# Pairwise products of features: tiles of 128 batch rows, stores of 31,744 B a partition, and the loads on ScalarE's queue

## The chip, the core and the metric

The kernel runs on one core of a Trainium2 chip. The metric is the device time of one execution in microseconds (us). The core has TensorE (PE; its weight loads are PEld), VectorE (DVE), ScalarE (ACT), GpSimd (POOL), SyncE (SP), and 16 DMA engines that move data between HBM and the on-chip memory. SBUF and PSUM have 128 partitions.

## The reference, cut to what matters

```python
# x: (B, F, E) = (2048, 32, 64) float32, W: (64, 64) float32
i_idx, j_idx = jnp.triu_indices(32, k=1)          # 496 pairs, i < j, i outermost
xw = jnp.einsum('bfe,ed->bfd', x, W)
y = xw[:, i_idx, :] * x[:, j_idx, :]              # (2048, 496, 64)
```

x has 16.8 MB and y has 260.0 MB. One batch row of y is 496 * 64 * 4 = 126,976 B.

## The kernel before

The 2048 batch rows are cut into 8 tiles of 256 rows; a partition holds two rows (`ROWS = 2`), row r * 128 + p of the tile for r = 0, 1. x_sb and xw_sb have two buffers each. The 496 pairs of a tile are cut into 16 chunks of 31 pairs, and `out_ring` has 8 slots of one chunk each: two rows of 31 * 64 * 4 = 7,936 B a partition, 2,031,616 B a slot.

SP issues every load and every store from one queue (lines 109 to 147). A load of a tile is three DMAs (line 112) for the features 0 to 7, 8 to 15 and 16 to 31 (`CUTS`): 2,048, 2,048 and 4,096 B in a row of x. The loads of tiles 0 and 1 come first; the load of tile t + 2 is issued behind the 16 stores of tile t. Each store (line 118) waits for the count `chunk_ready` and covers 256 stretches of 7,936 B in HBM. The first chunk of tile 0 is stored in two pieces (line 132), so that the first piece needs only part of x.

PE transposes two features at a time into PSUM (line 161), ACT copies that into `xT_sb` (line 202), PE multiplies it with W (line 174) and ACT copies the product into `xw_sb` (line 208), in groups of two features and two rows: 16 groups a tile. ACT also issues the two loads of W (line 221). After each tile but the first, ACT waits until VectorE has done the tile before, since xw_sb has two buffers.

VectorE multiplies (line 234): for each i, xw[i] broadcast over the features j > i, written into a slot of the ring. One instruction covers both rows; a chunk's end cuts an instruction in two. Before each chunk VectorE waits until the slot's last store has landed (`stored`).

Of the kernel before, what the change touches and what calls it, by code (L numbers as in the profile page):

```python
# [5 lines left out]
ALU = mybir.AluOpType  # L6
# [3 lines left out]
ROWS = 2  # L10
GROUP = 2
SLOTS = 8
CUTS = (0, 8, 16, 32)


def pair_pieces(F, chunk_pairs):

    chunks = [[] for _ in range(F * (F - 1) // 2 // chunk_pairs)]  # L20
    at = 0
    for i in range(F - 1):
        j = i + 1
        while j < F:
            place = at % chunk_pairs
            n = min(F - j, chunk_pairs - place)
            chunks[at // chunk_pairs].append((i, j, n, place))
            at += n
            j += n
    return chunks  # L30


def pairwise_interaction_kernel(nc: bass.Bass, x: bass.AP, W: bass.AP, out: bass.AP):
# [6 lines left out]


    B, F, E = x.shape
    PAIRS = F * (F - 1) // 2
    TILES = B // (LANES * ROWS)
    GROUPS = F // GROUP
    CHUNK = F - 1
    CHUNKS = PAIRS // CHUNK
    LAPS = CHUNKS // SLOTS
    PARTS = len(CUTS) - 1
    EARLY = CUTS[-2] - 1  # L50
    chunks = pair_pieces(F, CHUNK)
    assert B % (LANES * ROWS * 2) == 0 and PAIRS % CHUNK == 0 and CHUNKS % SLOTS == 0
    BANK = 512
    assert 2 * E == LANES and ROWS * GROUP * E <= BANK and F % GROUP == 0 and TILES >= 4
    assert CUTS[0] == 0 and CUTS[-1] == F and all(cut % GROUP == 0 for cut in CUTS)

    x_tiles = x.rearrange("(t r p) f e -> t p r f e", p=LANES, r=ROWS)
    out_tiles = out.rearrange("(t r p) q e -> t p r (q e)", p=LANES, r=ROWS)

    with ExitStack() as ctx:  # L60
# [6 lines left out]
        def sem(name):  # L67
            return ctx.enter_context(nc.semaphore(name))


        x_sb = [sb(f"x_sb{n}", [LANES, ROWS, F, E]) for n in range(2)]
        xw_sb = [sb(f"xw_sb{n}", [LANES, ROWS, F, E]) for n in range(2)]
        out_ring = [sb(f"out_ring{n}", [LANES, ROWS, CHUNK * E]) for n in range(SLOTS)]
        W_sb = sb("W_sb", [LANES, E])
        identity = sb("identity", [LANES, LANES])


        xT_sb = [sb(f"xT_sb{n}", [LANES, ROWS, GROUP // 2, LANES]) for n in range(2)]
        xT_ps = [psum(f"xT_ps{n}", [LANES, ROWS, GROUP // 2, LANES]) for n in range(2)]

        xw_bank = [[psum(f"xw_bank{n}_{odd}", [LANES, BANK]) for odd in range(2)] for n in range(2)]
        xw_ps = [[bank[:, 0:ROWS * GROUP // 2 * E].rearrange("p (r m e) -> p r m e", r=ROWS, e=E) for bank in banks]
                 for banks in xw_bank]
# [4 lines left out]
        x_landed = [[sem(f"x_landed{n}_{part}") for part in range(PARTS)] for n in range(2)]  # L88
# [5 lines left out]
        early_ready = sem("early_ready")  # L94
        early_stored = sem("early_stored")
        stored = [sem(f"stored{n}") for n in range(SLOTS)]

# [9 lines left out]
        @block.sync  # L107
        def _(sp):
            def load_x(t, buf):
                for part in range(PARTS):  # L110
                    f0, f1 = CUTS[part:part + 2]
                    sp.dma_start(x_sb[buf][:, :, f0:f1, :],  # L112
                                 x_tiles[t, :, :, f0:f1, :]).then_inc(x_landed[buf][part], 16)

            def store_chunk(t, c, skip=0):

                sp.wait_ge(chunk_ready, t * CHUNKS + c + 1)  # L117
                sp.dma_start(out_tiles[t, :, :, (c * CHUNK + skip) * E:(c + 1) * CHUNK * E],  # L118
                             out_ring[c % SLOTS][:, :, skip * E:]).then_inc(stored[c % SLOTS], 16)

            def store_then_load(k, buf, first=False):
                t = 2 * k + buf
                for c in range(CHUNKS):
                    store_chunk(t, c, skip=EARLY if first and c == 0 else 0)

                load_x(t + 2, buf)

            load_x(0, 0)
            load_x(1, 1)

            sp.wait_ge(early_ready, 1)
            sp.dma_start(out_tiles[0, :, :, 0:EARLY * E],
                         out_ring[0][:, :, 0:EARLY * E]).then_inc(early_stored, 16)
            for buf in range(2):
                store_then_load(0, buf, first=buf == 0)
            with sp.Fori(1, TILES // 2 - 1) as k:  # L136
                for buf in range(2):
                    store_then_load(k, buf)
            for t in range(TILES - 2, TILES):
                for c in range(CHUNKS):  # L140
                    store_chunk(t, c)

            sp.wait_ge(early_stored, 16)
            for slot in range(SLOTS):
                sp.wait_ge(stored[slot], 16 * TILES * LAPS)

        @block.tensor
        def _(pe):
            def tile(k, buf, first):
                t = 2 * k + buf  # L150

                def transpose_group(g):

                    if g * GROUP in CUTS:

                        pe.wait_ge(x_landed[buf][CUTS.index(g * GROUP)], 16 * (k + 1))
                    for r in range(ROWS):
                        for m in range(GROUP // 2):
                            f = g * GROUP + 2 * m
                            two = x_sb[buf][:, r, f:f + 2, :].rearrange("p f e -> p (f e)")  # L160
                            last = nc.tensor.transpose(xT_ps[g % 2][:, r, m, :], two, identity[:])  # L161
                    last.then_inc(transposed, 1)

                def project_group(g):

                    pe.wait_ge(xT_copied, t * GROUPS + g + 1)
                    if not (first and g < 2):

                        pe.wait_ge(xw_copied, 2 * (t * GROUPS + max(g - 1, 0)))
                    for r in range(ROWS):  # L170
                        for m in range(GROUP // 2):
                            for odd in range(2):
                                rows = slice(odd * E, (odd + 1) * E)
                                last = nc.tensor.matmul(xw_ps[g % 2][odd][:, r, m, :],  # L174
                                                        xT_sb[g % 2][rows, r, m, :], W_sb[rows, :],
                                                        start=True, stop=True)
                    last.then_inc(projected, 1)

                transpose_group(0)
                for g in range(GROUPS):  # L180
                    if g + 1 < GROUPS:
                        transpose_group(g + 1)
                    if first and g == 0:
                        pe.wait_ge(W_landed, 32)
                    project_group(g)

            pe.wait_ge(identity_ready, 1)
            for buf in range(2):
                tile(0, buf, first=buf == 0)
            with pe.Fori(1, TILES // 2) as k:  # L190
                for buf in range(2):
                    tile(k, buf, first=False)

        @block.scalar
        def _(act):
            def tile(k, buf, first):
                t = 2 * k + buf

                def copy_xT(g):

                    act.wait_ge(transposed, t * GROUPS + g + 1)
                    nc.scalar.copy(xT_sb[g % 2][:], xT_ps[g % 2][:]).then_inc(xT_copied, 1)  # L202

                def copy_xw(g):

                    act.wait_ge(projected, t * GROUPS + g + 1)
                    for odd in range(2):
                        nc.scalar.copy(xw_sb[buf][:, :, g * GROUP + odd:(g + 1) * GROUP:2, :],  # L208
                                       xw_ps[g % 2][odd]).then_inc(xw_copied, 1)

                copy_xT(0)
                for g in range(GROUPS):
                    if g + 1 < GROUPS:
                        copy_xT(g + 1)
                    copy_xw(g)
                if not first:

                    act.wait_ge(chunk_ready, t * CHUNKS)

            for odd in range(2):  # L220
                act.dma_start(W_sb[odd * E:(odd + 1) * E, :], W).then_inc(W_landed, 16)  # L221
            for buf in range(2):
                tile(0, buf, first=buf == 0)
            with act.Fori(1, TILES // 2) as k:
                for buf in range(2):
                    tile(k, buf, first=False)

        @block.vector
        def _(dve):
            def tile(k, buf, first):  # L230
                t = 2 * k + buf

                def multiply(slot, i, j, n, place):
                    return nc.vector.tensor_tensor(  # L234
                        slot[:, :, place:place + n, :],
                        xw_sb[buf][:, :, i:i + 1, :].to_broadcast([LANES, ROWS, n, E]),
# [54 lines left out]
```

## Time and profile before

| | |
|---|---|
| median of 3 runs | 672.33 us (672.03 to 672.47) |
| span of the profiled execution | 670.0 us |
| what lies around the span (median less span) | 2.3 us |
| VectorE busy | 562.1 us (84%) |
| PE busy | 211.4 us (32%) |
| ACT busy | 104.6 us (16%) |
| DMA, mean over the span | 413 GB/s |

The span runs from the first to the last instruction of the profiled execution; the profile gives this execution no other time of its own, so the runs' median stands for what lies around it. A window row of the trace gives, for a stretch of the span, each engine's busy time and number of instructions, TensorE's granted clock, the mean busy share of the 16 DMA engines and the rate at which they moved data. A share slightly above 1.00 means that packets of one engine overlap.

### The profile page before, as it was taken

How to read it: one execution, taken by the hardware profiler on the slowest of the kernel's cores; microseconds unless marked ns; L12 is line 12 of the kernel's file. 1: busy time of each engine (PE TensorE's matmuls, PEld its weight loads, DVE VectorE, ACT ScalarE, POOL GpSimd, SP SyncE). 2: the span in 40 equal slices, each digit the busy share in tenths (PEclk: the TensorE clock that was granted, in tenths of full speed). 3: DMA queues.
4: the chain of work that ended last, by engine and by line, in shares of the span. 5: the costliest groups of instructions: out<-in, count | busy, mean ns of one | idle time of the engine just before them, and what ended most of it. 6: DMA issues, size and time to landing. Idle time of an engine off the chain costs nothing.

```text
span 670.0 us, 4192 instructions
## 1 busy us (share of the span) xinstructions
PE 211.4 (32%) x1280; PEld 157.1 (23%) x1280; DVE 562.1 (84%) x362; ACT 104.6 (16%) x385; POOL 0.7 (0%) x6
## 2 busy tenths in 40 slices
PE   6995019400193001930029300392003910000000
PEld 4773017300173001720017200271002710000000
DVE  4999999999869997699977999779996899999800
ACT  3442004200042000410014100141001410000000
POOL 0000000000000000000000000000000000000000
DMA  8999999999999999999999999999999999999998
GB/s 318 422 416 419 418 360 427 425 427 429 381 426 426 426 429 373 426 428 428 427 382 428 426 429 427 382 427 427 429 425 396 428 426 428 425 420 419 419 420 342
DMA packets 41787, 277.00 MB, mean 413 GB/s; under 512 B 2608, under 2 KB 2608, under 8 KB 41776
## 3 DMA queue, kind: packets, MB, share of 16 engines
q1 hardware_dynamic: 41616, 276.83, 100.1%
q8 instruction: 5, 0.08, 0.0%
q10 hardware_dynamic: 160, 0.03, 0.0%
q14 instruction: 6, 0.05, 0.0%
HBM read 16.81 MB, written 260.05 MB: 413 GB/s over the span
## 4 chain that ended last, share of the span: by engine, by line
DMA 38%; SPq 29%; DVE 25%; issue 2%; DVEq 0%; PE 0%; ACTq 0%; ACT 0%
DMA out_dram<-out_ring 37%; DVE out_ring L234 25%; SPq L118 20%; SPq L112 8%; DMA W_sb<-in_W_dram 1%; DVEq L60 0%; SPq L117 0%; PE xw_bank L174 0%; ACTq L221 0%; ACT xw_sb L208 0%; SPq L136 0%; DVEq L250 0%; DVEq L267 0%; DVEq L242 0%; DVEq L254 0%
## 5 line engine op out<-in xcount | busy, mean ns | idle before, releaser
L234 DVE TENSOR_TENSOR out_ring<-xw_sb,x_sb 128x384 f32<-128x384 f32 (+11 forms) x362 | 562.1, 1615 | 73.6 <-DMA out_dram<-out_ring 64.3
L161 PE MATMUL xT_ps<-identity,x_sb 128*128 128x128 f32 x256 | 85.8, 444 | 325.7 <-DMA x_sb<-in_x_dram 325.7
L174 PE MATMUL xw_bank<-W_sb,xT_sb 64*128 64x64 f32 x1024 | 141.1, 430 | 1.9 <-DMA W_sb<-in_W_dram 1.2
L174 PEld LDWEIGHTS xw_bank<-W_sb,xT_sb 64*128 64x128 f32 x1024 | 118.7, 320 | 41.6 <-ACT xw_sb L208 25.4
L161 PEld LDWEIGHTS xT_ps<-identity,x_sb 128*128 128x128 f32 x256 | 38.4, 207 | 340.1 <-DMA x_sb<-in_x_dram 321.6
L202 ACT COPY xT_sb<-xT_ps 128x256 f32<-128x256 f32 x128 | 47.7, 373 | 344.7 <-PE xT_ps L161 344.2
L208 ACT COPY xw_sb<-xw_bank 128x128 f32<-128x128 f32 x256 | 55.6, 269 | 88.2 <-PE xw_bank L174 88.2
L202 ACT ACT_TABLE_LOAD x1 | 1.3, 1283 | 2.0 <-issue 2.0
L104 POOL TENSOR_SCALAR_AFFINE_SELECT identity<-identity 128x128 f32<-128x128 f32 x1 | 0.3, 294 | 0.2 <-POOL identity L102 0.2
L102 POOL MEMSET identity<- 128x128 f32 x1 | 0.2, 205 | 0.3 <-POOLq L279 0.3
L279 POOL MEMSET const-bfloat16-1.0<- 128x1 bf16 x1 | 0.1, 102 | 0.0
L279 POOL MEMSET const-uint8-127<- 128x1 uint8 x1 | 0.1, 102 | 0.0
L279 POOL MEMSET const-float32-0.0<- 128x1 f32 x1 | 0.1, 99 | 0.2 <-issue 0.2
L279 POOL MEMSET const-float32-1.0<- 128x1 f32 x1 | 0.1, 99 | 0.0
## 6 DMA issues: line engine op xcount, KB each, us to landing
out_dram<-out_ring SPq DMA_DIRECT2D x127, 1984.0 KB, 30.5
x_sb<-in_x_dram SPq DMA_DIRECT2D x16, 512.0 KB, 25.5
x_sb<-in_x_dram SPq DMA_DIRECT2D x8, 1024.0 KB, 22.7
out_dram<-out_ring SPq DMA_DIRECT2D x1, 1024.0 KB, 6.3
out_dram<-out_ring SPq DMA_DIRECT2D x1, 960.0 KB, 6.0
W_sb<-in_W_dram ACTq DMA_DIRECT2D x2, 16.0 KB, 5.4
```

The source lines that it names most:

```text
L102: nc.gpsimd.memset(identity[:], 0.0).then_inc(identity_zeroed, 1)
L104: nc.gpsimd.affine_select(out=identity[:], in_=identity[:], compare_op=ALU.not_equal, fill=1.0, base=0, pattern=[[-1, LANES]], channel_mul ...
L112: sp.dma_start(x_sb[buf][:, :, f0:f1, :], x_tiles[t, :, :, f0:f1, :]).then_inc(x_landed[buf][part], 16)
L118: sp.dma_start(out_tiles[t, :, :, (c * CHUNK + skip) * E:(c + 1) * CHUNK * E], out_ring[c % SLOTS][:, :, skip * E:]).then_inc(stored[c % S ...
L161: last = nc.tensor.transpose(xT_ps[g % 2][:, r, m, :], two, identity[:])
L174: last = nc.tensor.matmul(xw_ps[g % 2][odd][:, r, m, :], xT_sb[g % 2][rows, r, m, :], W_sb[rows, :], start=True, stop=True)
L202: nc.scalar.copy(xT_sb[g % 2][:], xT_ps[g % 2][:]).then_inc(xT_copied, 1)
L208: nc.scalar.copy(xw_sb[buf][:, :, g * GROUP + odd:(g + 1) * GROUP:2, :], xw_ps[g % 2][odd]).then_inc(xw_copied, 1)
L234: return nc.vector.tensor_tensor(slot[:, :, place:place + n, :], xw_sb[buf][:, :, i:i + 1, :].to_broadcast([LANES, ROWS, n, E]), x_sb[buf] ...
L279: nc = _bacc.Bacc("TRN2", target_bir_lowering=False, num_devices=1)
```

## The change

The batch is cut into 16 tiles of 128 rows, one row a partition. Rows are dealt to partitions differently: rows 2p and 2p + 1 of 256 go to partition p, so a load of 256 rows is 16,384 contiguous bytes a partition, and eight such loads (`LOADS`) fill four buffers (`XBUFS = 4`, eight tiles). The first load is two DMAs, one for each row of the pair. A tile's pairs are cut into 4 chunks of 124 pairs; the ring has 4 slots of 31,744 B a partition, and a store is 128 stretches of 31,744 B in HBM, whose starts lie 253,952 B apart. The stores stay on SP; all loads, the four at the start and the four later ones, are issued by ACT. A group is four features of one row (8 groups a tile). A multiply covers one row. PE waits for W before its first transpose; ACT raises `xw_copied` by 4 at the start so that PE's waits have one form. The piecewise start of the first chunk is gone. The loops of SP, ACT and VectorE are written out; PE's stays a loop.

```diff
-ROWS = 2
-GROUP = 2
-SLOTS = 8
-CUTS = (0, 8, 16, 32)
+ROWS = 2
+XBUFS = 4
+GROUP = 4
+CHUNKS = 4
+XW_PRIME = 4
...
-    x_tiles = x.rearrange("(t r p) f e -> t p r f e", p=LANES, r=ROWS)
-    out_tiles = out.rearrange("(t r p) q e -> t p r (q e)", p=LANES, r=ROWS)
+    x_loads = x.rearrange("(g p r) f e -> g p r f e", p=LANES, r=ROWS)
+    out_tiles = out.rearrange("(g p r) q e -> g r p (q e)", p=LANES, r=ROWS)
...
-        x_sb = [sb(f"x_sb{n}", [LANES, ROWS, F, E]) for n in range(2)]
-        xw_sb = [sb(f"xw_sb{n}", [LANES, ROWS, F, E]) for n in range(2)]
-        out_ring = [sb(f"out_ring{n}", [LANES, ROWS, CHUNK * E]) for n in range(SLOTS)]
+        x_sb = [sb(f"x_sb{n}", [LANES, ROWS, F, E]) for n in range(XBUFS)]
+        xw_sb = [sb(f"xw_sb{n}", [LANES, F, E]) for n in range(2)]
+        out_ring = [sb(f"out_ring{n}", [LANES, CHUNK * E]) for n in range(CHUNKS)]
...
         def _(sp):
+            for t in range(TILES):
+                g, r = divmod(t, ROWS)
                 for c in range(CHUNKS):
+                    sp.wait_ge(chunk_ready, t * CHUNKS + c + 1)
+                    sp.dma_start(out_tiles[g, r, :, c * CHUNK * E:(c + 1) * CHUNK * E],
+                                 out_ring[c][:]).then_inc(stored[c], 16)
...
         def _(act):
+            def load(g):
+                buf = g % XBUFS
+                if buf == 0:
                     for r in range(ROWS):
+                        act.dma_start(x_sb[0][:, r], x_loads[g, :, r]).then_inc(x_landed[0][r], 16)
+                else:
+                    act.dma_start(x_sb[buf][:], x_loads[g]).then_inc(x_landed[buf][0], 16)
...
+            for odd in range(2):
+                act.dma_start(W_sb[odd * E:(odd + 1) * E, :], W).then_inc(W_landed, 16)
+            for g in range(XBUFS):
+                load(g)
+            act.sem_inc(xw_copied, XW_PRIME)
+            for t in range(TILES):
+                copy_xT(t, 0)
+                if t >= 2:
+                    act.wait_ge(chunk_ready, (t - 1) * CHUNKS)
+                    done, r = divmod(t - 2, ROWS)
+                    if r == ROWS - 1 and done + XBUFS < LOADS:
+                        load(done + XBUFS)
                 for g in range(GROUPS):
                     if g + 1 < GROUPS:
+                        copy_xT(t, g + 1)
+                    copy_xw(t, g)
...
         def _(dve):
+            for t in range(TILES):
+                load, r = divmod(t, ROWS)
+                buf = load % XBUFS
                 for c in range(CHUNKS):
+                    if t > 0:
+                        dve.wait_ge(stored[c], 16 * t)
+                    slot = out_ring[c][:].rearrange("p (q e) -> p q e", e=E)
                     for i, j, n, place in chunks[c]:
+                        if i == 0 and r < len(x_landed[buf]):
+                            dve.wait_ge(x_landed[buf][r], 16 * (load // XBUFS + 1))
                         if i % GROUP == 0 and j == i + 1:
+                            dve.wait_ge(xw_copied, XW_PRIME + 2 * (t * GROUPS + i // GROUP + 1))
+                        last = nc.vector.tensor_tensor(
+                            slot[:, place:place + n, :], xw_sb[t % 2][:, i:i + 1, :].to_broadcast([LANES, n, E]),
+                            x_sb[buf][:, r, j:j + n, :], ALU.mult)
                     last.then_inc(chunk_ready, 1)
```

## Rows read from the trace of the kernel before

**Rows 1.** The page: span, and busy time of the engines (share of the span).

```profile
span 670.0 us, 4192 instructions
...
PE 211.4 (32%) x1280; PEld 157.1 (23%) x1280; DVE 562.1 (84%) x362; ACT 104.6 (16%) x385; POOL 0.7 (0%) x6
```

**Rows 2.** The page: all DMA packets, and the bytes read and written.

```profile
DMA packets 41787, 277.00 MB, mean 413 GB/s; under 512 B 2608, under 2 KB 2608, under 8 KB 41776
...
HBM read 16.81 MB, written 260.05 MB: 413 GB/s over the span
```

**Rows 3.** The chain that ended last, by engine.

```profile
DMA 38%; SPq 29%; DVE 25%; issue 2%; DVEq 0%; PE 0%; ACTq 0%; ACT 0%
```

**Rows 4.** Waits, all engines: total us, times, longest us.

```profile
DVE out_ring L234 <- DMA out_dram<-out_ring: 64.3, 89, 7.4
```

**Rows 5.** Windows without loads: last columns clock, DMA share, GB/s.

```profile
20.00:90.00 70.00, 39.15 (x242) 29.13 (x240) 70.00 (x46) 19.45 (x73) 0.00 (x0) 1.00 1.01 418
...
440.00:490.00 50.00, 16.43 (x104) 12.26 (x102) 46.93 (x34) 8.14 (x31) 0.00 (x0) 1.00 1.01 427
...
590.00:660.00 70.00, 0.00 (x0) 0.00 (x0) 42.04 (x33) 0.00 (x0) 0.00 (x0) 1.00 1.01 419
```

**Rows 6.** Windows around the six later loads.

```profile
90.00:100.00 10.00, 2.36 (x13) 1.85 (x14) 10.00 (x7) 0.83 (x3) 0.00 (x0) 1.00 0.98 322
170.00:180.00 10.00, 0.00 (x0) 0.00 (x0) 9.45 (x6) 0.00 (x0) 0.00 (x0) 1.00 0.99 353
250.00:270.00 20.00, 5.34 (x32) 4.06 (x32) 14.47 (x8) 2.36 (x8) 0.00 (x0) 1.00 1.00 383
340.00:350.00 10.00, 2.72 (x14) 1.94 (x14) 8.42 (x5) 1.18 (x4) 0.00 (x0) 1.00 0.97 356
420.00:430.00 10.00, 0.10 (x1) 0.10 (x2) 9.09 (x5) 0.00 (x0) 0.00 (x0) 1.00 0.98 349
500.00:510.00 10.00, 0.00 (x0) 0.00 (x0) 9.04 (x5) 0.00 (x0) 0.00 (x0) 1.00 0.98 379
```

**Rows 7.** Windows of one us, at the start, loads alone.

```profile
2.00:3.00 1.00, 0.00 (x0) 0.00 (x0) 0.00 (x0) 1.00 (x1) 0.00 (x0) 1.00 0.67 225
...
4.00:5.00 1.00, 0.00 (x0) 0.00 (x0) 0.00 (x0) 0.00 (x0) 0.00 (x0) 1.00 0.82 205
...
7.00:8.00 1.00, 0.51 (x6) 0.51 (x6) 0.00 (x0) 0.00 (x0) 0.00 (x0) 1.00 0.98 406
...
8.00:9.00 1.00, 1.00 (x8) 0.71 (x6) 0.00 (x0) 0.35 (x2) 0.00 (x0) 1.00 1.02 416
```

**Rows 8.** Windows of the start and of the end.

```profile
0.00:20.00 20.00, 13.60 (x82) 10.12 (x82) 10.88 (x6) 7.68 (x24) 0.70 (x6) 1.00 0.90 336
...
660.00:670.00 10.00, 0.00 (x0) 0.00 (x0) 0.00 (x0) 0.00 (x0) 0.00 (x0) 1.00 0.69 290
```

**Rows 9.** VectorE's multiplies, largest and a small form: busy, mean ns.

```profile
L234 DVE TENSOR_TENSOR out_ring<-xw_sb,x_sb 128x3968 f32<-128x3968 f32 x7 | 30.0, 4290 | 1.3 <-DMA out_dram<-out_ring 1.3
...
L234 DVE TENSOR_TENSOR out_ring<-xw_sb,x_sb 128x384 f32<-128x384 f32 x32 | 17.7, 554 | 3.8 <-DMA out_dram<-out_ring 3.8
```

**Rows 10.** Timeline of the start: start us, us, engine, line.

```profile
0.74 1.19 ACTq L221 DMA_DIRECT2D W_sb<-in_W_dram  x2
...
0.75 3.67 SPq L112 DMA_DIRECT2D x_sb<-in_x_dram  x6
...
1.96 1.28 ACT L202 ACT_TABLE_LOAD   x1 [1.96 <-issue]
...
5.21 1.09 PE L161 MATMUL xT_ps<-identity,x_sb 128*128 128x128 f32 x4 [5.21 <-DMA x_sb<-in_x_dram]
...
9.12 16.37 DVE L234 TENSOR_TENSOR out_ring<-xw_sb,x_sb 128x896 f32<-128x896 f32 x8 [9.12 <-ACT xw_sb L208]
```

**Rows 11.** One line's instructions, L118: the stores' issue.

```profile
L118 SPq DMA_DIRECT2D out_dram<-out_ring x128: 372/4201/9513, 13.6 to 637.5; - x128
```

**Rows 12.** The page's DMA issues: KB each, us to landing.

```profile
out_dram<-out_ring SPq DMA_DIRECT2D x127, 1984.0 KB, 30.5
```

More of the change, by code:

```diff
@@ L43, in pairwise_interaction_kernel @@
     PAIRS = F * (F - 1) // 2
-    TILES = B // (LANES * ROWS)
+    TILES = B // LANES
+    LOADS = TILES // ROWS
     GROUPS = F // GROUP
[L46 to L50, printed above, removed]
-    chunks = pair_pieces(F, CHUNK)
[L52 to L55, printed above, removed]
-    x_tiles = x.rearrange("(t r p) f e -> t p r f e", p=LANES, r=ROWS)
-    out_tiles = out.rearrange("(t r p) q e -> t p r (q e)", p=LANES, r=ROWS)
+    HALF = GROUP // 2
+    CHUNK = PAIRS // CHUNKS
+    LAP = XBUFS * ROWS
+    chunks = pair_pieces(F, CHUNK)
+    assert B % (LANES * ROWS) == 0 and PAIRS % CHUNKS == 0 and TILES % LAP == 0
+    assert 2 * E == LANES and F % GROUP == 0 and GROUP % 2 == 0 and GROUPS % 2 == 0
+    x_loads = x.rearrange("(g p r) f e -> g p r f e", p=LANES, r=ROWS)
+    out_tiles = out.rearrange("(g p r) q e -> g r p (q e)", p=LANES, r=ROWS)
     with ExitStack() as ctx:
@@ L87, in pairwise_interaction_kernel @@
         identity_ready = sem("identity_ready")
-        x_landed = [[sem(f"x_landed{n}_{part}") for part in range(PARTS)] for n in range(2)]
+        x_landed = [[sem(f"x_landed{n}_{r}") for r in range(ROWS if n == 0 else 1)] for n in range(XBUFS)]
         transposed = sem("transposed")
@@ L93, in pairwise_interaction_kernel @@
         chunk_ready = sem("chunk_ready")
-        early_ready = sem("early_ready")
-        early_stored = sem("early_stored")
-        stored = [sem(f"stored{n}") for n in range(SLOTS)]
+        stored = [sem(f"stored{n}") for n in range(CHUNKS)]
         block = ctx.enter_context(nc.Block())
@@ L108, in _ @@
         def _(sp):
[L109 to L119, printed above, removed]
@@ L121, in store_then_load @@
-            def store_then_load(k, buf, first=False):
-                t = 2 * k + buf
-                for c in range(CHUNKS):
[L124 to L145, printed above, removed]
+            for t in range(TILES):
+                g, r = divmod(t, ROWS)
+                for c in range(CHUNKS):
+                    sp.wait_ge(chunk_ready, t * CHUNKS + c + 1)
+                    sp.dma_start(out_tiles[g, r, :, c * CHUNK * E:(c + 1) * CHUNK * E],
+                                 out_ring[c][:]).then_inc(stored[c], 16)
@@ L147, in _ @@
+            for slot in range(CHUNKS):
+                sp.wait_ge(stored[slot], 16 * TILES)
         @block.tensor
         def _(pe):
[L149 to L156, printed above, removed]
-                    for r in range(ROWS):
[L158 to L169, printed above, removed]
-                    for r in range(ROWS):
[L171 to L179, printed above, removed]
@@ new lines, in transpose_group, with project_group @@
+            def transpose_group(buf, r, g):
+                for m in range(HALF):
+                    f = g * GROUP + 2 * m
+                    two = x_sb[buf][:, r, f:f + 2, :].rearrange("p f e -> p (f e)")
+                    last = nc.tensor.transpose(xT_ps[g % 2][:, m, :], two, identity[:])
+                last.then_inc(transposed, 1)
+            def project_group(t, g):
+                pe.wait_ge(xT_copied, t * GROUPS + g + 1)
+                pe.wait_ge(xw_copied, XW_PRIME + 2 * (t * GROUPS + g - 1))
+                for m in range(HALF):
+                    for odd in range(2):
+                        rows = slice(odd * E, (odd + 1) * E)
+                        last = nc.tensor.matmul(xw_ps[g % 2][odd][:, m, :], xT_sb[g % 2][rows, m, :], W_sb[rows, :],
+                                                start=True, stop=True)
+                last.then_inc(projected, 1)
@@ new lines, in _ @@
+            pe.wait_ge(identity_ready, 1)
+            pe.wait_ge(W_landed, 32)
+            with pe.Fori(0, TILES // LAP) as k:
+                for buf in range(XBUFS):
+                    for r in range(ROWS):
+                        t = k * LAP + (buf * ROWS + r)
+                        if r < len(x_landed[buf]):
+                            pe.wait_ge(x_landed[buf][r], 16 * (k + 1))
+                        transpose_group(buf, r, 0)
+                        for g in range(GROUPS):
+                            if g + 1 < GROUPS:
+                                transpose_group(buf, r, g + 1)
+                            project_group(t, g)
@@ L180, in tile @@
                 for g in range(GROUPS):
                     if g + 1 < GROUPS:
[L182 to L226, printed above, removed]
@@ L228, in _ @@
+                        copy_xT(t, g + 1)
+                    copy_xw(t, g)
         @block.vector
         def _(dve):
[L230 to L236, printed above, removed]
-                        x_sb[buf][:, :, j:j + n, :], ALU.mult)
-                for c in range(CHUNKS):
-                    if not (first and c < SLOTS):
-                        dve.wait_ge(stored[c % SLOTS], 16 * (t * LAPS + c // SLOTS))
-                    if first and c == SLOTS:
-                        dve.wait_ge(early_stored, 16)
-                    slot = out_ring[c % SLOTS][:].rearrange("p r (q e) -> p r q e", e=E)
+            for t in range(TILES):
+                load, r = divmod(t, ROWS)
+                buf = load % XBUFS
+                for c in range(CHUNKS):
+                    if t > 0:
+                        dve.wait_ge(stored[c], 16 * t)
+                    slot = out_ring[c][:].rearrange("p (q e) -> p q e", e=E)
@@ L247, in tile @@
                     for i, j, n, place in chunks[c]:
+                        if i == 0 and r < len(x_landed[buf]):
+                            dve.wait_ge(x_landed[buf][r], 16 * (load // XBUFS + 1))
                         if i % GROUP == 0 and j == i + 1:
-                            dve.wait_ge(xw_copied, 2 * (t * GROUPS + i // GROUP + 1))
-                        if i == 0:
-                            for part in range(PARTS):
-                                dve.wait_ge(x_landed[buf][part], 16 * (k + 1))
-                                if first or part == PARTS - 1:
-                                    n = CUTS[part + 1] - j
-                                    last = multiply(slot, i, j, n, place)
-                                    j, place = j + n, place + n
-                                    if first and part == PARTS - 2:
-                                        last.then_inc(early_ready, 1)
-                        else:
-                            last = multiply(slot, i, j, n, place)
@@ L263, in tile @@
-                    last.then_inc(chunk_ready, 1)
-            for buf in range(2):
-                tile(0, buf, first=buf == 0)
-            with dve.Fori(1, TILES // 2) as k:
-                for buf in range(2):
-                    tile(k, buf, first=False)
+                            dve.wait_ge(xw_copied, XW_PRIME + 2 * (t * GROUPS + i // GROUP + 1))
+                        last = nc.vector.tensor_tensor(
+                            slot[:, place:place + n, :], xw_sb[t % 2][:, i:i + 1, :].to_broadcast([LANES, n, E]),
+                            x_sb[buf][:, r, j:j + n, :], ALU.mult)
```

20 lines of the change are left out of this document (15 added, 5 removed).

## The prediction

> **What bounds the kernel now.** I read the page first: VectorE is the busiest engine with 562.1 of 670.0 us, and PE and ACT are far below [rows 1]. Then the DMA part: 277.0 MB cross the engines at a mean of 413 GB/s [rows 2]. The chain of waits puts most of the span on DMA and on SP's queue, which holds stores that can't be issued yet, and 25% on VectorE [rows 3]. The waits decide between the two: VectorE stood still 64.3 us in 89 waits for a landed store [rows 4], so stores free the slots too late, and not the other way round. Last come windows of the DMA rate. Where no load runs it is flat: 427 GB/s in five stretches of 50 to 60 us between 100 and 580 us (one is shown), and 418 and 419 GB/s while the first and the last tile are stored [rows 5]. The DMA share is 1.01 there. The reader is to see that the kernel is bound by bytes, and where it moves them below its own best rate. There are three such places. Around the six later loads the rate falls to 322 to 383 GB/s [rows 6]; against 427 the six windows lack 1.05 + 0.74 + 0.88 + 0.71 + 0.78 + 0.48 = 4.64 MB, which is 10.9 us. The first 20 us lack (427 - 336) * 20 = 1.82 MB, 4.3 us, and the last 10 us 137 * 10 = 1.37 MB, 3.2 us [rows 8]. The bytes of the change are the same, so its time is again bytes by rate, plus start and end.
>
> **The later loads.** Before, a load of 2.1 MB is half packets of 4,096 B and half of 2,048 B. In the first microseconds loads run alone, the small ones first: 225 and 205 GB/s at 2 to 5 us, then 406 and 416 at 7 to 9 us [rows 7]. So I put the dips of rows 6 down to the small packets: if 1.05 MB goes at 411 GB/s, the mean of those two rows (2.6 us), and the load costs 4.9 + 10.9 / 6 = 6.7 us in all, the small half takes 4.1 us, about 255 GB/s, which fits the start. The new loads are 16,384 B a partition, longer than any load packet here. At 416 GB/s the four later ones lack 8.4 MB * (1/416 - 1/427) = 0.5 us. This part gives 10.9 - 0.5 = -10.4 us. Bounds: all 10.9, or, if dips come from reads among writes and not from packet size, four dips of 1.8 us stay and only 3.6 us are won. I take the upper end, since the 4,096 B row is the nearest in size. That ACT issues these loads costs nothing that shows: a DMA takes SP 0.37 to 9.5 us to issue [rows 11], ACT would hold for that long once in two tiles, and behind it wait the group copies of one tile, PE's projections and, a tile later, VectorE. Per 128 rows ACT has 104.6 / 16 = 6.5 us and PE 211.4 / 16 = 13.2 us of work [rows 1] in a period of 40 us, so 26 us of cover remain. Four buffers put a load's issue six tiles (240 us) ahead of its use. The wait of ACT for the tile before last is the old one; it now stands in front of the load.
>
> **The stores' packets.** A store has the same bytes in a quarter of the packets: 31,744 B for four of 7,936. No row has such a packet. The two nearest sizes give a line: 4,096 B at 411 GB/s on 16 engines are 159.5 ns, 7,936 B at 427 are 297.4 ns [rows 5, 7]; the slope is 35.9 ps a byte and 12.4 ns are left for a packet whatever its size. Four old packets take 1,189 ns, a new one by this line 1,152, which is 441 GB/s; by the other bound nothing changes. The first point is a load and the second a store, so the line mixes two directions, and I take half: 1,171 ns, 434 GB/s. The stores take 65.0 MB (two eighths) at 418.5 and 195.0 MB at 427, 155.3 + 456.8 = 612.1 us; 1.56% of that is -9.6 us, bounds 0 and -19.1. I keep the lower rate of the first and last tile, for which the rows show no cause.
>
> The Trainium skill prices the same term: "DMA: Bandwidth & Descriptors", section "Why small descriptors are slow (HBM only)", gives about 3 cycles of overhead for each packet beside one cycle for 32 B. By it, as an estimate, four packets of 248 + 3 cycles become one of 992 + 3, 0.9%, and this term would be -5.5 us and the total 656 us; the line through the rows has more than twice that overhead.
>
> **Start.** Before, loads ran from 0.75 us on SP beside W on ACT, and the first multiply began at 9.12 us [rows 10]. Now ACT issues W twice and then the five load DMAs. At 0.6 us each (its two took 1.19 us) the first row of x is issued by 2.5 us and ACT is free at 5 us, after its table load (1.3 us) at 6.3. Data began to flow about 0.65 us behind the first issue's end before (SP's six took 3.67 us, so the first ended near 1.35; 225 GB/s from 2.0) [rows 7, 10], so I take 3.2 us now. The first 1.05 MB takes 2.5 us; with 1 us to land x is there at 6.8. From the first transpose to the first multiply 3.9 us passed before, 1.2 of them a wait for W, which now comes first: VectorE begins near 10. Its first chunk takes 8.7 us (below), so the first store's data move at about 21. The loads, 8.4 MB at 416 GB/s, last until 3.2 + 20.2 = 23.4 us. So the two more tiles that are loaded at the start cover the longer first chunk, and the piecewise first store is not missed; without this cover each late microsecond would cost one. In the first 20 us the lack is 3.2 * 427 + 16.8 * 11 = 1.55 MB, 3.6 us for 4.3: -0.6 us, with 2 us either way.
>
> **VectorE.** A multiply costs 154 ns and 1.042 ns an element (4,290 ns for 3,968, 554 for 384) [rows 9]. The sum of busy time, 562.1 us for 362 instructions and 507,904 elements [rows 1], leaves 0.09 us for one, since neighbours overlap. Now a tile has 31 multiplies and three cuts: 34 * 0.09 + 31,744 * 1.042 = 36.2 us, 16 * 36.2 = 579 us, 17 us more than before. A chunk takes 8.7 to 9.8 us. The DMA needs 16.25 MB / 434 + 1.05 / 416 = 40.0 us a tile, so 3.8 us of VectorE's idle time a tile hide this. The four slots have the bytes of the old eight. A slot's round is fill (9.8), issue and the store's own move (9.4), some 20 us, against four chunk times of 10, so the queue holds two or three stores; 17 us of lateness would have to come up before the engines run dry.
>
> **End.** The last stores are bound by the engines as before; a last store twice as long has no row that makes it cost, 0 to 2 us, and I take 0.
>
> **Sum.** 670.0 - 10.4 - 9.6 - 0.6 = 649.4 us of span; with the 2.3 us by which the median of the runs stands above the span, 651.7, so 652 us.
>
> **The rivals.**
> *No gain from longer packets.* The line through rows 5 and 7 mixes a load with a store, and the store's rate may hang on something else. Then 670.0 - 10.4 - 0.6 + 2.3 = 661 us.
> *The dips stay.* Loads among stores cost 1.8 us each whatever their packets. For: the first of the dips lacks 1.05 MB where the six lack 0.77 on the mean, with the same packets [rows 6]. Against: loads without stores show the same low rate while their small packets run, and 406 to 416 GB/s after that [rows 7]. Four loads then cost 6.8 us more than I count: 659 us, or 668 with the first rival.
> *Stores become slower by where they go.* The starts of a store's stretches lie twice as far apart, 253,952 B, and an engine writes each for four times as long. For: the rate does hang on the place or the time, 418 against 427 GB/s with packets of one size [rows 5]. Against: nothing else in the rows. If all stores ran at 418.5 without a packet gain, 621.4 us instead of 612.1, the time would be 671; at twice that deficit, 410 GB/s, 634.3 us, it is 684 us. It ends slower than before from about 417 GB/s downwards. The Trainium skill, in "DMA: Bandwidth & Descriptors", section "Latency and other measured facts", reports copies that lose up to half their rate when the row pitch is a large power of two; 253,952 B is not one, so by it no loss is due, and no row here shows such a pitch.
> *The four slots starve the engines.* A store that lands over 17 us late would do it. Stores land 30.5 us after issue now, but with six or seven in the queue [rows 12]. Each us of hole in a tile would be 16 us: 668 and more.
>
> **How the numbers follow.** My forecast, 645 to 657 us, has 0.56; no packet gain 0.15; dips that stay 0.12; slower stores 0.08; starving slots 0.03; faster than 645, up to the whole line (642 us), 0.06. The range 644 to 664 us reaches from just above the whole line to past both 659 and 661 and holds about 0.8. A measurement of this kernel can tell a change from about 0.2% (1.3 us) on. Faster by more than that: the forecast, the two partial rivals and the last case, 0.88; within it 0.04 (all stores at 418.5, or a small hole in each tile); slower 0.08.
>
> **What would show it.** The windows of the changed kernel show 430 GB/s or more without loads, and none under 400 between 25 and 640 us. The DMA part lists some 8,192 store packets. VectorE is busy about 579 us in 544 instructions and still waits for landed stores, some 60 us in all. The loads land long before their tile. The first multiply begins near 10 us, and the rate has no hole between 20 and 30 us. The prediction is wrong if stores run below 425 GB/s, if the dips are still there, if more store packets are listed than rows, or if VectorE waits for ACT's copies in the middle of the span.

## The result, and the profile of the changed kernel

The changed kernel takes 655.62 us (655.25 to 655.73 in four runs) against 672.3 us: a ratio of 0.9754, 95% interval 0.974 to 0.9768. The forecast was 652 us, 644 to 664.

The page of the changed kernel: span, busy time, and the DMA queues with packets, MB and share.

```profile
span 653.8 us, 3891 instructions
...
PE 209.3 (32%) x1280; PEld 157.5 (24%) x1280; DVE 570.5 (87%) x544; ACT 101.8 (16%) x385; POOL 0.7 (0%) x6
...
DMA packets 10828, 277.00 MB, mean 424 GB/s; under 512 B 1344, under 2 KB 1344, under 8 KB 1344
...
q1 hardware_dynamic: 9216, 260.05, 92.4%
q10 hardware_dynamic: 1600, 16.81, 6.3%
q8 instruction: 5, 0.08, 0.0%
q14 instruction: 7, 0.06, 0.0%
```

The reader is to see that the bytes are those of [rows 2] in a quarter of the packets: SP's queue (q1) has 9,216, which are 64 stores of 128 packets of 31,744 B and 16 small ones each. VectorE is busy 570.5 us in 544 instructions, 8 us more than in [rows 1].

The windows of the start, of three stretches without loads and of the end (the last two columns are DMA share and GB/s):

```profile
0.00:20.00 20.00, 12.59 (x78) 9.54 (x80) 9.77 (x6) 7.17 (x23) 0.70 (x6) 1.00 0.86 351
20.00:30.00 10.00, 9.87 (x61) 7.14 (x59) 10.00 (x8) 4.96 (x19) 0.00 (x0) 1.00 1.02 393
100.00:130.00 30.00, 12.80 (x80) 9.85 (x80) 29.31 (x30) 6.26 (x24) 0.00 (x0) 1.00 1.01 433
420.00:480.00 60.00, 19.20 (x119) 14.52 (x120) 57.03 (x59) 9.67 (x37) 0.00 (x0) 1.00 1.00 432
590.00:630.00 40.00, 0.00 (x0) 0.00 (x0) 33.36 (x33) 0.00 (x0) 0.00 (x0) 1.00 1.00 432
638.00:646.00 8.00, 0.00 (x0) 0.00 (x0) 0.00 (x0) 0.00 (x0) 0.00 (x0) 1.00 0.98 421
646.00:652.00 6.00, 0.00 (x0) 0.00 (x0) 0.00 (x0) 0.00 (x0) 0.00 (x0) 1.00 0.14 58
```

These answer to [rows 5] and [rows 8]. Without loads the rate is 432 to 433 GB/s from the third tile of the new 128 rows to the last. Before, it was 427, and 418 to 419 in the first and the last tile. At the end it falls to 58 GB/s at a share of 0.14 for six microseconds: the work of some two of the 16 engines.

The windows around the four later loads, which answer to [rows 6]:

```profile
75.00:105.00 30.00, 13.08 (x80) 9.84 (x80) 30.00 (x29) 6.26 (x24) 0.00 (x0) 1.00 1.00 429
145.00:175.00 30.00, 13.08 (x80) 9.85 (x80) 26.00 (x26) 6.26 (x24) 0.00 (x0) 1.00 0.99 423
225.00:250.00 25.00, 13.08 (x80) 9.84 (x80) 20.29 (x24) 6.26 (x24) 0.00 (x0) 1.00 1.00 430
310.00:335.00 25.00, 13.08 (x80) 9.84 (x80) 20.97 (x22) 6.26 (x24) 0.00 (x0) 1.00 1.00 425
```

Against 433 GB/s they lack 0.12 + 0.30 + 0.08 + 0.20 = 0.70 MB, 1.6 us in all, 0.4 us a load where it was 1.8.

The timeline of the start, as in [rows 10], and VectorE's wait for landed stores, as in [rows 4]:

```profile
0.74 1.20 ACTq L162 DMA_DIRECT2D W_sb<-in_W_dram  x2
...
1.98 1.08 ACTq L147 DMA_DIRECT2D x_sb<-in_x_dram  x2
3.08 1.88 ACTq L149 DMA_DIRECT2D x_sb<-in_x_dram  x3
...
7.29 1.12 PE L113 MATMUL xT_ps<-identity,x_sb 128*128 128x128 f32 x4 [7.29 <-DMA x_sb<-in_x_dram]
...
10.23 2.23 DVE L196 TENSOR_TENSOR out_ring<-xw_sb,x_sb 128x1984 f32<-128x1984 f32 x1 [10.23 <-ACT xw_sb L158]
```

```profile
DVE out_ring L196 <- DMA out_dram<-out_ring: 44.5, 39, 4.2
```

The first multiply begins at 10.2 us, and VectorE still waits for the stores, 44.5 us.

### The profile page after: what moved, and what is told of

Its sections match the earlier page's. It is cut to its first block, busy times and chain, and to the rows that moved or that the text cites. A ratio compares the mean times of both kernels' runs of the same rounds, so it can differ in the third digit from the quotient of the medians.

```text
span 653.8 us, 3891 instructions
## 1 busy us (share of the span) xinstructions
PE 209.3 (32%) x1280; PEld 157.5 (24%) x1280; DVE 570.5 (87%) x544; ACT 101.8 (16%) x385; POOL 0.7 (0%) x6
## 3 DMA queue, kind: packets, MB, share of 16 engines
q1 hardware_dynamic: 9216, 260.05, 92.4%
HBM read 16.81 MB, written 260.05 MB: 423 GB/s over the span
## 4 chain that ended last, share of the span: by engine, by line
DMA 60%; DVE 33%; issue 2%; PE 0%; ACTq 0%; DVEq 0%; ACT 0%
DMA out_dram<-out_ring 59%; DVE out_ring L196 33%; DMA x_sb<-in_x_dram 1%; ACTq L162 0%; PE xw_bank L123 0%; PE xT_ps L113 0%; DVEq L54 0%; ACT xw_sb L158 0%; DVEq L195 0%
## 5 line engine op out<-in xcount | busy, mean ns | idle before, releaser
L196 DVE TENSOR_TENSOR out_ring<-xw_sb,x_sb 128x256 f32<-128x256 f32 (+27 forms) x544 | 570.5, 1123 | 54.8 <-DMA out_dram<-out_ring 44.5
L123 PE MATMUL xw_bank<-W_sb,xT_sb 64*128 64x64 f32 x1024 | 138.9, 429 | 343.9 <-ACT xT_sb L153 341.9
L113 PE MATMUL xT_ps<-identity,x_sb 128*128 128x128 f32 x256 | 83.7, 442 | 7.3 <-DMA x_sb<-in_x_dram 7.3
## 6 DMA issues: line engine op xcount, KB each, us to landing
x_sb<-in_x_dram ACTq DMA_DIRECT2D x4, 1024.0 KB, 11.5
```

Source lines behind the costliest of these rows:

```text
L113: last = nc.tensor.transpose(xT_ps[g % 2][:, m, :], two, identity[:])
L123: last = nc.tensor.matmul(xw_ps[g % 2][odd][:, m, :], xT_sb[g % 2][rows, m, :], W_sb[rows, :], start=True, stop=True)
L196: last = nc.vector.tensor_tensor(slot[:, place:place + n, :], xw_sb[t % 2][:, i:i + 1, :].to_broadcast([LANES, n, E]), x_sb[buf][:, r, j:j ...
```

## The experiments

All kernels compute the whole reference. The edits are shown without the declarations and wait counts that follow from them. Times are medians; beside each stands the ratio to the kernel before with its 95% interval, from runs on the same chip. The kernel before took 671.9 to 672.3 us beside the several experiments, so a difference from the changed kernel's 655.62 us is good to some 0.4 us.

### Store packets of 7,936 and of 15,872 B

```diff
-CHUNKS = 4
+CHUNKS = 16
```

> The changed kernel with 16 chunks of 31 pairs, so that a store is 128 packets of 7,936 B and all else (places in HBM, loads, tiles, bytes of the ring) stays. Theory A, that the stores' rate is set by a cost per packet: the rate without loads falls from 433 to about 427 GB/s, 600.6 to 609 us of stores, and the time rises from 655.6 to 664 to 667 us. Rival, that the rate rose with the dealing of rows and the new places: it stays at 433 and the time within 1 us of 655.6. On the end of the run: if one DMA engine has fallen behind over the run, the last 6 to 7 us in which a single engine moves data are still there; if the end is long because the last store and its packets are long, it shrinks to about 3 us.

Measured: 666.8 us (0.9922, 0.9906 to 0.9939), 11.2 us more than the changed kernel. Its windows, in the order: without loads early and late, around the second and third of the four later loads, and the end:

```profile
100.00:130.00 30.00, 10.60 (x68) 8.28 (x69) 30.00 (x40) 5.70 (x23) 0.00 (x0) 1.00 1.01 426
420.00:480.00 60.00, 18.71 (x116) 14.15 (x118) 58.40 (x75) 9.67 (x37) 0.00 (x0) 1.00 1.01 419
150.00:175.00 25.00, 13.08 (x80) 9.85 (x80) 24.34 (x31) 6.26 (x24) 0.00 (x0) 1.00 1.01 403
230.00:255.00 25.00, 13.08 (x80) 9.84 (x80) 19.25 (x22) 6.26 (x24) 0.00 (x0) 1.00 1.01 406
655.00:665.00 10.00, 0.00 (x0) 0.00 (x0) 0.00 (x0) 0.00 (x0) 0.00 (x0) 1.00 0.81 336
```

The rate without loads is 426 GB/s again: the gain is that of the packets, and the rival falls. From 400 us on it is 419. The four later loads lack 0.27 + 0.58 + 0.50 + 0.55 = 1.9 MB in windows of 25 or 30 us (two are shown), 4.4 us, for packets of 16,384 B on ACT's queue: with short stores the dips are there. The end is short: 336 GB/s over the last ten microseconds, so the view that one late engine costs its 6 us whatever the packets does not hold. SP's issue of a store is held up again, as in [rows 11]; in the changed kernel it takes 0.33 us each time:

```profile
L101 SPq DMA_DIRECT2D out_dram<-out_ring x256: 332/2058/6025, 12.5 to 638.9; - x128
```

```diff
-CHUNKS = 4
+CHUNKS = 8
```

> The changed kernel with 8 chunks of 62 pairs: store packets of 15,872 B. A fixed cost per packet: the four-fold packets were worth 11 us from 7,936 to 31,744 B, three packets in four; one more packet in 31,744 B gives back a third, 3.7 us: 659 us. If instead what matters is that no more than four stores of nine descriptors an engine are queued, SP's issue time and the end tell: issue near 0.33 us and a single engine 6 us behind at the end as in the changed kernel, or issue of some us and an end of 2 to 3 us as with 7,936 B; then the gain is not proportional to the packets, 656 or 667 us.

Measured: 658.7 us (0.9805, 0.9789 to 0.9822), 3.1 us more than the changed kernel; early and late windows:

```profile
100.00:130.00 30.00, 12.00 (x76) 9.28 (x78) 30.00 (x34) 6.26 (x24) 0.00 (x0) 1.00 1.01 430
420.00:480.00 60.00, 21.56 (x132) 16.11 (x132) 57.40 (x64) 10.94 (x43) 0.00 (x0) 1.00 1.01 427
```

SP's issue takes 0.33 us here too, so a full queue is not what sets the rate. Three packet lengths now lie on a line. On 16 engines 7,936 B at 426 GB/s take 298.1 ns and 31,744 B at 433 take 1,173.0; the slope is 36.75 ps a byte and 6.5 ns are left for a packet (the rates are rounded to 1 GB/s, which leaves some 0.9 ns either way). For 15,872 B this gives 589.8 ns or 430.6 GB/s, and 430 is measured. The slope alone is 435 GB/s, the ceiling that the Trainium skill ("DMA: Bandwidth & Descriptors", section "Specifications") states for the fabric; trace and page agree.

### The same with the batch rows in the reverse order

```diff
-out_tiles[g, r, :, ...], x_loads[g]
+out_tiles[LOADS - 1 - g, r, :, ...], x_loads[LOADS - 1 - g]
```

> One look at the kernel with store packets of 7,936 B and the batch rows taken from the last to the first. In its forward form the rate was 426 GB/s up to some 300 us and 419 from 400 us to the end. If the lower rate hangs on the place in HBM, it comes first now and 426 last; if on the time or the program, it stays in the second half. The time is 667 us within 2 either way.

Measured: 666.5 us in one run; early and late windows:

```profile
100.00:130.00 30.00, 10.68 (x68) 8.32 (x69) 30.00 (x40) 5.78 (x23) 0.00 (x0) 1.00 1.01 426
420.00:480.00 60.00, 19.46 (x120) 14.70 (x120) 58.41 (x74) 9.87 (x39) 0.00 (x0) 1.00 1.01 419
```

The lower rate stays in the second half, so it does not hang on the place in HBM. In time per packet it is 303.0 ns for 298.1 at 7,936 B, 594.7 for 590.6 at 15,872 B (427 GB/s) and 1,175.7 for 1,173.0 at 31,744 B (432): 3 to 5 ns for a packet, whatever its length, so that long packets dilute it. Nor does it hang on the time alone. In the records of single packets the median of a store's packet steps by 5 ns: from 300 to 305 ns in the last tile of the kernel before, from 1,175 to 1,180 ns near 500 us in the changed kernel, but not at all after 100 us in the kernels with small load packets, with the loads on SP or with two buffers of x (all below). What sets it was not found.

### The rows dealt as before

```diff
-x.rearrange("(g p r) f e -> g p r f e", ...)
-out.rearrange("(g p r) q e -> g r p (q e)", ...)
+x.rearrange("(g r p) f e -> g p r f e", ...)
+out.rearrange("(g r p) q e -> g r p (q e)", ...)
```

> The changed kernel with the batch rows dealt as before (row r * 128 + p of 256 to partition p): the stretches of a store lie 126,976 B apart and a load is two packets of 8,192 B instead of one of 16,384. If the new places have no weight for the rate: 655.6 within 1.5 us (the four later loads may cost some tenths more). If they brought part of the gain, the rate without loads falls below 433 GB/s; each GB/s is 1.4 us.

Measured: 655.8 us (0.976, 0.9745 to 0.9774). The places have no weight that shows.

### Four kernels on the loads

Small packets for the four later loads, on ACT's queue:

```diff
-load(done + XBUFS)
+load_cut(done + XBUFS)      # three DMAs: features 0 to 7, 8 to 15, 16 to 31
```

> The changed kernel, whose four later loads are cut by features again into packets of 2,048, 2,048 and 4,096 B; still on ACT's queue and equally early. If the dips of before came from the small packets, four dips of 1.8 us come back for four of 0.4 us: 5 to 6 us more, 661 us. If they came from the loads standing in one queue with the stores, nothing changes (655.6 within 0.7).

Measured: 656.7 us (0.9773, 0.9757 to 0.9789), 1.1 us more, and the interval overlaps that of the changed kernel (0.974 to 0.9768). The last 15 us of the changed kernel and of this one:

```profile
638.80:653.80 15.00, 0.00 (x0) 0.00 (x0) 0.00 (x0) 0.00 (x0) 0.00 (x0) 1.00 0.50 216
640.10:655.10 15.00, 0.00 (x0) 0.00 (x0) 0.00 (x0) 0.00 (x0) 0.00 (x0) 1.00 0.39 169
```

The longer end alone is (216 - 169) * 15 = 0.71 MB, 1.6 us. The windows that hold the changed kernel's four later loads run at 428 to 434 GB/s here, where they run at 423 to 430 there: small load packets on ACT's queue make no dip. They do arrive otherwise than before, spread over some 60 us a load where the kernel before moves a load in 10.

All loads of x on SP, the later ones behind the stores:

```diff
+                if r == ROWS - 1 and g + XBUFS < LOADS:
+                    load(g + XBUFS)                       # in SP's program
```

> The changed kernel with all loads of x issued by SP, the later ones behind the stores of the two tiles whose buffer they fill. If the issuing queue is without weight, the time is that of the changed kernel within 1 us. If loads on a queue of their own are what removed the dips, four dips of 1.8 us come back: 661 us.

Measured: 656.3 us (0.9767, 0.9751 to 0.9783), 0.7 us more. Here too the end is longer, 163 GB/s over the last 15 us for 216, 1.8 us.

Both edits together:

> The changed kernel with the two load edits of the first runs together: the later loads are cut into packets of 2,048, 2,048 and 4,096 B, and all loads are issued by SP, the later ones behind the stores of the tiles whose buffer they fill. Alone the small packets cost 1.1 us and SP's queue 0.7 us. If it takes both to make the dips (small loads that an engine meets one after another, with no store beside them), four dips of 1.8 us come back: 661 to 664 us. If the dips of before had another cause, the two add up: 657 to 658 us.

Measured: 658.7 us (0.9801, 0.9785 to 0.9817), 3.1 us more: more than the sum of the two, but half of what the prediction's cause would give, and 2.4 us of it lie in the end (148 GB/s over the last 15 us).

The other way round, the kernel before with long loads alone:

```diff
-    "(t r p) f e -> t p r f e", "(t r p) q e -> t p r (q e)"
+    "(t p r) f e -> t p r f e", "(t p r) q e -> t p r (q e)"
...
-                load_x(t + 2, buf)
+                sp.dma_start(x_sb[buf][:], x_tiles[t + 2]).then_inc(x_landed[buf][PARTS - 1], 16)
```

> The kernel before with one part of the change alone: rows 2p and 2p + 1 go to partition p, and each of the six later loads is one DMA of 16,384 B a partition instead of three with packets of 2,048 and 4,096 B; still on SP, behind the stores, which keep their 7,936 B. If small load packets make the dips, as the prediction has it, 10 us are won: 662 us. If a load among stores of 7,936 B costs its 1.2 us whatever its own packets, as the four loads of the changed kernel did with stores of 7,936 B, some 4 us are won: 668 us.

Measured: 669.6 us (0.9964, 0.9951 to 0.9976), 2.4 us less than before. The windows are those of [rows 6], from an execution that took 1.2 us more than the median:

```profile
90.00:100.00 10.00, 0.00 (x0) 0.00 (x0) 10.00 (x7) 0.00 (x0) 0.00 (x0) 1.00 0.99 344
170.00:180.00 10.00, 0.00 (x0) 0.00 (x0) 9.94 (x6) 0.00 (x0) 0.00 (x0) 1.00 1.03 387
250.00:270.00 20.00, 2.84 (x16) 2.00 (x16) 14.38 (x8) 1.18 (x4) 0.00 (x0) 1.00 1.01 400
340.00:350.00 10.00, 0.46 (x2) 0.46 (x3) 8.06 (x5) 0.00 (x0) 0.00 (x0) 1.00 0.98 366
420.00:430.00 10.00, 0.00 (x0) 0.00 (x0) 9.23 (x5) 0.00 (x0) 0.00 (x0) 1.00 1.01 367
500.00:510.00 10.00, 0.00 (x0) 0.00 (x0) 9.14 (x5) 0.00 (x0) 0.00 (x0) 1.00 1.03 386
```

Against 427 they lack 3.39 MB, 7.9 us, where 10.9 us were lacking: long load packets remove 3 us of the dips. So four kernels put a load's price at 1.8 us (before), 1.3 (long load packets), 1.1 (on ACT's queue as well, in the kernel with 7,936 B stores) and 0.4 (long stores as well). In this order the largest single step is the stores' packets, not the loads'; in another order the steps were not measured.

### Two buffers of x

```diff
-XBUFS = 4
+XBUFS = 2
```

> The changed kernel with two buffers of x (four tiles) instead of four. The start then has 4.2 MB of loads instead of 8.4, done near 13 us, and the first store's data move from 21 us on. If the loads of the two more buffers are what covers the long first chunk: a hole of 7 us, 662 to 663 us, and nothing else changes, since a load is still two tiles (80 us) early. If VectorE makes the hole up in the first tiles: within 1 us of 655.6.

Measured: 660.8 us (0.9837, 0.982 to 0.9853), 5.2 us more. The windows from 12 to 20 us, around the last load, and at the end:

```profile
12.00:16.00 4.00, 4.00 (x28) 3.10 (x28) 4.00 (x3) 1.97 (x7) 0.00 (x0) 1.00 0.40 172
16.00:20.00 4.00, 4.00 (x30) 3.10 (x29) 4.00 (x4) 1.90 (x8) 0.00 (x0) 1.00 0.29 127
470.00:500.00 30.00, 13.16 (x80) 9.82 (x80) 22.56 (x23) 6.25 (x24) 0.00 (x0) 1.00 1.00 416
643.80:658.80 15.00, 0.00 (x0) 0.00 (x0) 0.00 (x0) 0.00 (x0) 0.00 (x0) 1.00 0.66 286
```

The changed kernel moves 430 and 426 GB/s in these two windows; the hole is (430 - 172 + 426 - 127) * 4 us = 2.2 MB, 5.1 us, and VectorE does not make it up. That it equals the whole loss is chance. Two buffers also mean six later loads for four; the two further ones, near 400 and 480 us, lack 0.7 MB, 1.6 us, and the end is shorter, 286 GB/s over the last 15 us for 216, which gives 2.4 us back.

### Three kernels on the end

The last store in two parts:

```diff
+                    for p0, p1 in ((0, 104), (104, 128)) if end else ((0, 128),):
+                        sp.dma_start(out_tiles[g, r, p0:p1, ...], out_ring[c][p0:p1, :]).then_inc(stored[c], 16)
```

> The changed kernel whose very last store is two DMAs, partitions 0 to 103 and 104 to 127. With 13 and 12 engines for the two, engines 0 to 11 would get two packets more than now and three engines none. If the end waits for one engine that is late and it is among the three spared, the time falls by 4 us to 651.5; if it is late but another, or if all engines are alike, it rises by 2.3 us to 658.

Measured: 665.6 us (0.9907, 0.989 to 0.9923), 10 us more, which neither view expected. Its windows before and in the end:

```profile
610.00:630.00 20.00, 0.00 (x0) 0.00 (x0) 15.01 (x21) 0.00 (x0) 0.00 (x0) 1.00 1.00 432
640.00:650.00 10.00, 0.00 (x0) 0.00 (x0) 0.00 (x0) 0.00 (x0) 0.00 (x0) 1.00 0.80 222
656.00:662.00 6.00, 0.00 (x0) 0.00 (x0) 0.00 (x0) 0.00 (x0) 0.00 (x0) 1.00 0.11 48
```

With the two partial stores in the queues the rate is 222 GB/s at a share of 0.80, against 432 at 1.00 with whole ones: the packets take longer by half and more (single ones up to 2.7 us for 1.18). The run says nothing of which engine is late.

More program, on an engine for which nobody waits:

```diff
+            for c in range(TILES * CHUNKS - 8):
+                pool.wait_ge(chunk_ready, c + 1)
+                for n in range(16):
+                    nc.gpsimd.memset(spare[:, 16 * c + n:16 * c + n + 1], 0)
```

> The changed kernel with 896 memsets of one byte a partition on GpSimd, 16 after each of the first 56 chunks; nothing waits for them. They add some 57 KB of instructions to fetch. If the late engine is late because it fetches the program (0.3 to 0.9 us a packet, and slower stores behind it), it falls 3 to 6 us further behind: 659 to 661 us. If its lateness has another cause: 655.6 within 0.7.

Measured: 657.7 us (0.979, 0.9773 to 0.9806), 2.1 us more, below what was expected. Its instruction queues:

```profile
q8 instruction: 5, 0.08, 0.0%
q14 instruction: 14, 0.11, 0.0%
```

Seven packets more than in the changed kernel, all of 8 KB; at 0.3 us each they come to 2.1 us. That this is the measured difference is chance, as the part on the end below shows.

Less program: W twice on the diagonal of a 128 by 128 tile, so that one product serves two features:

```diff
-                    for odd in range(2):
-                        rows = slice(odd * E, (odd + 1) * E)
-                        last = nc.tensor.matmul(xw_ps[g % 2][odd][:, m, :], xT_sb[g % 2][rows, m, :], W_sb[rows, :],
-                                                start=True, stop=True)
+                    last = nc.tensor.matmul(xw_ps[g % 2][:, 2 * m:2 * m + 2, :].rearrange("p f e -> p (f e)"),
+                                            xT_sb[g % 2][:, m, :], W_sb[:], start=True, stop=True)
```

> The changed kernel with W twice on the diagonal of a 128 by 128 tile of zeros: one product for two features instead of two, one copy for a group instead of two. TensorE's program shrinks from 2,560 executed instructions to 1,536 and ScalarE loses 128 copies; the same result, the same bytes of x and y. If the end waits for an engine that fetches the program's packets, five of 16 KB (0.9 us) go down to two or three, as they did with two buffers of x, and 2 us are won: 653.5 us. If the late engine is late for another reason: 655.6 within 0.7, since TensorE and ScalarE are not waited for.

Measured: 653.3 us (0.9723, 0.9709 to 0.9736), 2.3 us less than the changed kernel, and the fastest of all. Its busy times, granted clock, instruction queues, and windows late and at the end:

```profile
PE 128.3 (20%) x768; PEld 116.5 (18%) x768; DVE 570.3 (88%) x544; ACT 88.1 (14%) x257; POOL 0.8 (0%) x7
...
PEclk9857575756557565575655757556575755655555
...
q8 instruction: 3, 0.05, 0.0%
q14 instruction: 6, 0.05, 0.0%
```

```profile
420.00:480.00 60.00, 16.27 (x96) 14.81 (x96) 57.13 (x59) 10.93 (x32) 0.00 (x0) 0.60 1.00 433
636.00:644.00 8.00, 0.00 (x0) 0.00 (x0) 0.00 (x0) 0.00 (x0) 0.00 (x0) 0.50 1.01 436
644.00:650.00 6.00, 0.00 (x0) 0.00 (x0) 0.00 (x0) 0.00 (x0) 0.00 (x0) 0.50 0.43 185
```

Three packets of instructions fewer (two of 16 KB), 146 executed instructions a tile for 218, and the end is shorter: 185 GB/s over the last six microseconds of data for 58. The rate before that is the same, 433.

## Why the prediction was right, and where not

**What bounds it.** Right: bytes by rate. The measured terms, from the rows above, are 670.0 - 9.3 (dips, 10.9 to 1.6) - 11.5 (stores) + 0.4 (start) + 4.0 (end) = 653.6 us of span; 653.8 was measured, and the runs' median lies 1.8 us above. That they meet so closely is in part luck: 1 GB/s, to which the windows are rounded, is 1.4 us of the stores.

**The stores' packets.** Right, and mis-sized by 1.9 us. The line from a load and a store gave 12.4 ns a packet and the prediction took half, 6.2; the runs give 6.5. The rest comes from the first and the last tile, whose lower rate the prediction kept: with 433 GB/s throughout, 260.05 MB take 600.6 us for 612.1. The estimate from the Trainium skill for this term, -5.5 us, is too small by half; that its total, 656, lies nearer is chance, since the end (4.0 us), the dips (1.1) and the start (1.0) were missed in the other direction.

**The later loads.** The size was right (-10.4 forecast, -9.3 measured), the cause named was not. The prediction put the dips down to load packets of 2,048 B, by way of the start, where such loads run alone. Small packets put back into the changed kernel cost 1.1 us instead of 5 to 6, none of it around the loads, and long ones put into the kernel before bring 2.4 us instead of 10. The dips shrink by three edits of this change together, and most by the longer store packets, which the prediction had in another term. The rival that dips stay whatever the packets is nearer to the truth for the kernel before, and did not come true because the stores changed too. Why a load costs less beside long store packets was not tried further. That the forecast came so near for this term is therefore luck.

**The start.** Right: 3.6 us lacking in the first 20 us were forecast against 427 GB/s, and 351 GB/s give (427 - 351) * 20 = 1.52 MB, 3.6 us. The loads of the two further buffers do cover the long first chunk; without them a hole of 5.1 us opens. What was missed is a dip between 20 and 30 us, 0.9 us, where the first store meets the last loads.

**VectorE.** Right in kind: it is hidden. It took 570.5 us for the 579 forecast, and waits 44.5 us for stores where some 60 were forecast.

**The end.** This term was missed: "0 to 2 us, and I take 0". It costs 4.0 us more than before, since engines that have kept pace stand idle for six microseconds while the last finish. Shorter store packets shorten it (the last ten microseconds run at 336 GB/s with 7,936 B). A smaller program shortens it too and a larger one lengthens it, by 2.3 and 2.1 us, which is also about the time of the instruction packets that these kernels have fewer or more. The view behind the two runs was therefore that one engine fetches the program and falls behind with its share of every store. The packet records speak against it. On a full engine a data packet starts 3 to 4 ns before the one ahead of it ends, so from 32 us on the records can be strung into 16 chains, one an engine. In the changed kernel the last chain ends at 652.84 us, the next at 650.38, and twelve of them at 645.3 to 646.9. None of the 11 instruction packets after 32 us lies on the last chain. With more program the last chain ends at 654.67 us; the seven further packets all lie on another, which ends at 649.12.

What sets the last chain apart is the time of its store packets. In the 13 us in which TensorE works on a tile they take some 1.20 to 1.24 us for 1.175, tile after tile until TensorE's work ends at 560 us, and from 352 us on no other chain shows this. There it adds up to 0.62 us a tile in the changed kernel, 0.77 with GpSimd's memsets and 0.43 with one product for two features. The compute engines execute 218, 282 and 146 instructions a tile in the three, so it is 2.7 to 3.0 ns for each. One DMA engine thus pays for executed instructions, not for fetched ones as far as the records show them. Why it does, and why short packets leave less of it at the end, stays open.

**The other rivals.** Slower stores by their place: excluded by the kernel with the rows dealt as before, 655.8 us. Starving slots: excluded, the rate without loads has no holes.

## What to carry to other kernels

When the DMA engines are full, price a change in packet length by two lengths of the same direction in the trace; in this kernel the length of the stores' packets also changed how much a load disturbed them. A dip that coincides with a kind of packet is not yet caused by it: put that packet alone into the other kernel before it goes into a sum, and read the windows of that run and not its time alone: two runs here had their loss in another place. That a difference has the size of a suspected cost does not show the cause either: follow the packets. Look at the last ten microseconds as a term of its own, since a slightly late engine costs nothing until there is no more work for the others.

## What was not expected of the hardware

- Two DMAs of 104 and 24 partitions in place of one of 128 ran at 222 GB/s for 432 while they were in the queues, and cost 10 us for 4 MB.
- One DMA engine of the 16 moved its store packets more slowly while the core's compute engines executed a tile's instructions, by 2.7 to 3.0 ns for each instruction in three kernels; the cause is open.
- In the second half of the changed kernel and of most of its variants a store packet takes 3 to 5 ns more, whatever its length and in the reversed order too; four variants never show it there. The cause is open.
- With W on the diagonal TensorE was granted a lower clock: 0.9 in the first slice of the span and 0.5 to 0.8 in the slices after; 1.0 is the higher of its two levels (2.4 GHz) and 0.5 the lower (1.2). It worked for some 8 us in every 38 us there, and for 13 us in the changed kernel, where it was granted 1.0 throughout, as in the kernel before. It cost nothing that shows, since PE is busy 20% of the span and nobody waits for it.
